# Making the head of the Fourier stage inside the channel MLP's stage

## The reference, cut to what matters

```
x = shortcut + window_attention(ln(x))
x = x + gelu(ln(x) @ fc1_w + fc1_b) @ fc2_w + fc2_b          # channel MLP
g = group_norm(x, 32 groups)                                 # per image: mean, variance, (g - m) / sqrt(s + 1e-5)
f = rfft2(g)                                                 # per image, over the 16 x 16 tokens
o1 = softshrink(f times the complex block weights w1 + b1)   # 8 blocks of 24 channels
o2 = softshrink(o1 times w2 + b2)
x = x + irfft2(o2) + g
```

## Time and profile before

| | us |
|---|---|
| median of 3 runs | 1169.13 |
| lowest and highest run | 1167.31, 1169.83 |
| span of the profiled execution | 1161.7 |
| PE busy in that span | 1005.0 (87%) |

### The profile page before, as it was taken

The page is one execution under the profiler, slowest core; times in us unless marked ns, Lnnn a source line. Parts: engine busy times, 40 slices in busy tenths (PEclk is TensorE's granted clock), DMA queues, the critical chain, the costliest instruction groups (busy, mean ns, idle before and its releaser), DMA issues. The chain is left out here.

```text
span 1161.7 us, 20448 instructions
## 1 busy us (share of the span) xinstructions
PE 1005.0 (87%) x7506; PEld 763.8 (66%) x7507; DVE 574.7 (49%) x1388; ACT 424.4 (37%) x859; POOL 286.9 (25%) x399
## 2 busy tenths in 40 slices
PE   6895999999699699899799659999849799975996
PEld 5685778787465578688698526666637455554675
DVE  4753555653311475456566743444458477642221
ACT  3655155555232223344352111111127276731332
POOL 4454320110100112100001344555412211111242
PEclk9885899999799899899898869999969899985998
DMA  8543763320011120200004611112144433125660
GB/s 91 118 124 120 166 149 80 93 69 3 1 41 62 42 59 1 55 1 2 1 1 119 191 34 41 49 45 52 25 123 108 125 110 93 48 86 200 207 202 14
DMA packets 103286, 91.58 MB, mean 79 GB/s; under 512 B 25873, under 2 KB 95063, under 8 KB 102558
## 3 DMA queue, kind: packets, MB, share of 16 engines
q1 hardware_dynamic: 90953, 75.58, 24.3%
q0 software_dynamic: 5632, 11.07, 3.6%
q10 hardware_dynamic: 6613, 3.74, 1.1%
HBM read 64.44 MB, written 29.70 MB: 81 GB/s over the span
## 5 line engine op out<-in xcount | busy, mean ns | idle before, releaser
L1224 DVE TENSOR_REDUCE l0a_nmax<-l0a_psS 98x2 f32<-98x392 f32 x96 | 54.4, 567 | 55.1 <-PE l0a_psS L1039 51.0
L868 DVE TENSOR_REDUCE l3a_nmax<-l3a_psS 128x2 f32<-128x512 f32 x96 | 62.0, 685 | 31.6 <-PE l3a_psS L722 31.6
L2665 ACT ACTIVATE l2e_H<-l2e_psH 128x512 f32<-128x512 f32 x40 | 21.7, 594 | 129.3 <-PE l2e_psH L2627 129.3
L824 ACT ACTIVATE l3a_PT<-l3a_psST 128x512 f32<-128x512 f32 x96 | 54.6, 596 | 28.7 <-PE l3a_psST L752 28.2
L1174 ACT ACTIVATE l0a_PT<-l0a_psST 98x392 f32<-98x392 f32 x96 | 47.2, 497 | 42.1 <-PE l0a_psST L1081 41.8
L2645 PEld LDWEIGHTS l2e_psY<-W2T,l2e_HT 128*128 128x128 f32 x320 | 51.5, 190 | 15.9 <-issue 15.7
L2588 POOL DMA_INDIRECT ys<-l2e_Y,result_of x40 | 42.0, 1051 | 71.3 <-DVE l2e_Y L2692 65.2
L2645 PE MATMUL l2e_psY<-W2T,l2e_HT 128*128 x320 | 57.3, 332 | 1.3 <-DVE l2e_Y L2692 0.8
L2624 PE MATMUL l2e_psH<-W1T,l2e_XT 128*128 x80 | 41.3, 640 | 2.8 <-issue 2.0
L2583 POOL DMA_INDIRECT l2e_X<-xn,token_at x40 | 39.3, 983 | 17.1 <-issue 17.1
L2692 DVE COPY l2e_Y<-l2e_psY 128x384 f32<-128x384 f32 x20 | 11.2, 558 | 65.1 <-PE l2e_psY L2645 65.1
(11 more groups left out here) (559 smaller groups left out, 2699.9 us busy)
## 6 DMA issues: line engine op xcount, KB each, us to landing
l3w_A<-in_w SPq DMA_DIRECT2D x8, 771.0 KB, 5.4
l3w_B<-in_w SPq DMA_DIRECT2D x8, 672.0 KB, 5.4
l3a_QS<-qd SPq DMA_DIRECT2D x72, 64.0 KB, 2.3
l3a_KS<-kd SPq DMA_DIRECT2D x72, 64.0 KB, 2.3
rd<-l0q_r_p SPq DMA_DIRECT2D x24, 168.0 KB
l0a_QS<-qd SPq DMA_DIRECT2D x54, 64.0 KB
l0a_KS<-kd SPq DMA_DIRECT2D x54, 64.0 KB
W2T<-in_w2t SPq DMA_DIRECT2D x2, 1536.0 KB, 16.9
```

The source lines that it names most:

```text
L824: nc.scalar.activation(PT[n % 3][:, s, :], psST[item % 2][:, :], ACT.Exp).then_inc(exp_done, 1)
L868: nc.vector.tensor_reduce(nmax[k % 2][:, TI * u:TI * (u + 1), s], psS[item % 2][:, :].rearrange("p (t k) -> p t k", t=TI), AX.X, ALU.max, ...
L1224: mx = nc.vector.tensor_reduce(nmax[k % 2][0:WQ, 2 * j:2 * (j + 1), s], psS[item % 2][0:WQ, 0:2 * W0].rearrange("p (t k) -> p t k", t=2), ...
```

## The change

A class `FourierFront` now owns the tiles and semaphores of the group norm (sums, squares, XC, SQ, XN and so on, names l1g_...), of the block weights and of the constant rows. It lives in a stage of its own around the MLP and the Fourier stage, so its tiles keep their places across the barrier. Its methods have the operations of before, unchanged in form. The MLP's stage calls them for pair 0, with its own psT tiles for the products of mean and variance; the Fourier stage calls them for the later pairs only.

```diff
-def l0_mlp(nc, G, w):
+def l0_mlp(nc, G, w, gn, w_next):
...
         def _(sp):
+            gn.load_weights(sp, w_next)
             for p in range(NP - 1):
...
         def _(pool):
+            gn.clear_weights()
             for p in range(NP):
...
                 nc.gpsimd.tensor_tensor(X, X, free(b2[:, 0:1], [0, 4], [1, C]), ALU.add).then_inc(x_biased, 1)
+                if p == 1:
+                    gn.negate_weights(pool)
...
                 first(p)
                 if p + 1 < NP:
                     norm(p + 1)
+                if p == NP - 2:
+                    pe.wait_ge(xT_done, 2 * NP)
+                    gn.mean(pe, psT[0], 0)
+                if p == NP - 1:
+                    gn.variance(pe, psT[1], 0)
                 second(p)
...
                 hidden(p)
                 if p + 1 < NP:
                     norm(p + 1)
+                if p == NP - 2:
+                    gn.square(act, 0)
+                    gn.square(act, 1)
+            gn.root(act, 0)
...
                 if p + 1 < NP:
                     norm(p + 1)
+                if p == NP - 2:
+                    gn.total(dve, 0, (x_in, 16))
+                    gn.centre(dve, psT[0], 0)
+                if p == NP - 1:
+                    gn.square_total(dve, 0)
+                    gn.with_eps(dve, psT[1], 0)
+                    gn.scale(dve, 0)
+                    gn.norm(dve, 0)
                 for a in range(2):
...
+                if p == 0:
+                    gn.constant_rows()
```

More of the change, by code:

```diff
@@ L1259, in _, with __init__, clear_weights, load_weights @@
                         stats.vector(nc, dve, 2 * p + a, a, (x_added, 2 * p + a + 1))
+class FourierFront:
+    def __init__(self, st, G):
+        self.nc, self.G, self.st = st.nc, G, st
+        self.ones = G["afno"]["ones"]
+        two = lambda name, shape: [st.sb(f"{name}{u}", shape) for u in range(2)]
+        self.sums, self.squares = st.sb("sums", [P, 2, GROUPS]), st.sb("squares", [P, 2, GROUPS])
+        self.var, self.std, self.rstd = (st.sb(n, [P, 2, GROUPS]) for n in ("var", "std", "rstd"))
+        self.XC, self.SQ, self.XN = two("XC", [P, TI, C]), two("SQ", [P, TI, C]), two("XN", [P, TI, C])
+        self.sum_done, self.mean_mm, self.xc_done, self.sq_done, self.square_done = st.sems("sum_done mean_mm xc_done sq_done square_done")
+        self.var_mm, self.eps_done, self.std_done, self.rstd_done, self.xn_done = st.sems("var_mm eps_done std_done rstd_done xn_done")
+        R = CH + 1
+        self.W1, self.W2, self.lam = st.sb("W1", [R, 2, 3, CH]), st.sb("W2", [R, 2, 3, CH]), st.sb("lam", [CH, 1])
+        self.FX, self.C1 = st.sb("FX", [R, 2, 2, 2 * NF]), st.sb("C1", [R, 2, 2, 2 * NF])
+        self.w_zeroed, self.w_in, self.negated, self.rows_set = st.sems("w_zeroed w_in negated rows_set")
+    def clear_weights(self):
+        self.nc.gpsimd.memset(self.W1[:], 0.0).then_inc(self.w_zeroed, 1)
+        self.nc.gpsimd.memset(self.W2[:], 0.0).then_inc(self.w_zeroed, 1)
+        self.nc.gpsimd.memset(self.lam[:, :], -LAMBDA).then_inc(self.negated, 1)
+    def load_weights(self, sp, w):
+        W1, W2, R = self.W1, self.W2, CH + 1
+        sp.wait_ge(self.w_zeroed, 2)
+        for n in range(NB):
+            a, k = n // 4, n % 4
+            r = slice(k * BS, (k + 1) * BS)
+            of_block = lambda ap: rows(ap, n * BS * BS, [BS, BS], [NB * BS * BS, 2], [1, BS])
+            sp.dma_start(W1[r, a, 1:3, r], of_block(w["w1"])).then_inc(self.w_in, 16)
+            sp.dma_start(W2[r, a, 1:3, r], of_block(w["w2"])).then_inc(self.w_in, 16)
+        for a in range(2):
+            sp.dma_start(W1[CH:R, a, 1:3, :], rows(w["b1"], a * CH, [C, 1], [C, 2], [1, CH])).then_inc(self.w_in, 16)
+            sp.dma_start(W2[CH:R, a, 1:3, :], rows(w["b2"], a * CH, [C, 1], [C, 2], [1, CH])).then_inc(self.w_in, 16)
+    def negate_weights(self, pool):
+        pool.wait_ge(self.w_in, 16 * (2 * NB + 4))
+        for W in (self.W1, self.W2):
+            self.nc.gpsimd.tensor_scalar(W[:, :, 0, :], W[:, :, 2, :], -1.0, None, ALU.mult).then_inc(self.negated, 1)
+    def constant_rows(self):
+        R, V = CH + 1, self.nc.vector
+        V.memset(self.FX[CH:R, :, :, 0:NF], 1.0).then_inc(self.rows_set, 1)
+        V.memset(self.FX[CH:R, :, :, NF:], 0.0).then_inc(self.rows_set, 1)
+        V.memset(self.C1[CH:R, :, 0, :], 1.0).then_inc(self.rows_set, 1)
+        V.memset(self.C1[CH:R, :, 1, :], 0.0).then_inc(self.rows_set, 1)
+    def mean(self, pe, psM, p):
+        pe.wait_ge(self.sum_done, 2 * p + 2)
+        if p:
+            pe.wait_ge(self.xc_done, 2 * p)
+        self.nc.tensor.matmul(psM[:, 0:2 * GROUPS], self.ones[:, :], self.sums[:, :, :].rearrange("p u g -> p (u g)"), start=True, stop=True).then_inc(self.mean_mm, 1)
+    def variance(self, pe, psV, p):
+        pe.wait_ge(self.square_done, 2 * p + 2)
+        if p:
+            pe.wait_ge(self.eps_done, p)
+        self.nc.tensor.matmul(psV[:, 0:2 * GROUPS], self.ones[:, :], self.squares[:, :, :].rearrange("p u g -> p (u g)"), start=True, stop=True).then_inc(self.var_mm, 1)
+    def square(self, act, i):
+        act.wait_ge(self.xc_done, i + 1)
+        if i >= 2:
+            act.wait_ge(self.square_done, i - 1)
+        self.nc.scalar.activation(self.SQ[i % 2][:], self.XC[i % 2][:], ACT.Square).then_inc(self.sq_done, 1)
+    def root(self, act, p):
+        act.wait_ge(self.eps_done, p + 1)
+        self.nc.scalar.activation(self.std[:], self.var[:], ACT.Sqrt).then_inc(self.std_done, 1)
+    def total(self, dve, p, *ready):
+        for sem, value in ready:
+            dve.wait_ge(sem, value)
+        if p:
+            dve.wait_ge(self.mean_mm, p)
+        for u in range(2):
+            X = self.G["X"][:, TI * (2 * p + u), 0:1]
+            self.nc.vector.tensor_reduce(self.sums[:, u, :], free(X, [GC, GROUPS], [C, TI], [1, GC]), AX.XY, ALU.add).then_inc(self.sum_done, 1)
+    def spread(self, ap):
+        return free(ap, [0, TI], [1, GROUPS], [0, GC])
+    def in_groups(self, ap):
+        return ap.rearrange("p t (g c) -> p t g c", g=GROUPS)
+    def centre(self, dve, psM, p):
+        dve.wait_ge(self.mean_mm, p + 1)
+        for u in range(2):
+            X = self.G["X"][:, TI * (2 * p + u):TI * (2 * p + u + 1), :]
+            self.nc.vector.tensor_tensor(self.in_groups(self.XC[u][:]), self.in_groups(X), self.spread(psM[:, u * GROUPS:u * GROUPS + 1]), ALU.subtract).then_inc(self.xc_done, 1)
+    def square_total(self, dve, p):
+        if p:
+            dve.wait_ge(self.var_mm, p)
+        for u in range(2):
+            dve.wait_ge(self.sq_done, 2 * p + u + 1)
+            self.nc.vector.tensor_reduce(self.squares[:, u, :], free(self.SQ[u][:, 0, 0:1], [GC, GROUPS], [C, TI], [1, GC]), AX.XY, ALU.add).then_inc(self.square_done, 1)
+    def with_eps(self, dve, psV, p):
+        dve.wait_ge(self.var_mm, p + 1)
+        self.nc.vector.tensor_scalar(self.var[:], psV[:, 0:2 * GROUPS].rearrange("p (u g) -> p u g", u=2), 1e-5, None, ALU.add).then_inc(self.eps_done, 1)
+    def scale(self, dve, p):
+        V, std, var, rstd = self.nc.vector, self.std, self.var, self.rstd
+        dve.wait_ge(self.std_done, p + 1)
+        V.reciprocal(rstd[:], std[:]).then_inc(self.rstd_done, 1)
+        dve.wait_ge(self.rstd_done, 4 * p + 1)
+        V.tensor_tensor(std[:], rstd[:], rstd[:], ALU.mult).then_inc(self.rstd_done, 1)
+        dve.wait_ge(self.rstd_done, 4 * p + 2)
+        V.scalar_tensor_tensor(std[:], std[:], -0.5, var[:], ALU.mult, ALU.mult).then_inc(self.rstd_done, 1)
+        dve.wait_ge(self.rstd_done, 4 * p + 3)
+        V.scalar_tensor_tensor(rstd[:], std[:], 1.5, rstd[:], ALU.add, ALU.mult).then_inc(self.rstd_done, 1)
+        dve.wait_ge(self.rstd_done, 4 * p + 4)
+    def norm(self, dve, p, *ready):
+        for u in range(2):
+            for sem, value in ready:
+                dve.wait_ge(sem, value(2 * p + u))
+            self.nc.vector.tensor_tensor(self.in_groups(self.XN[u][:]), self.in_groups(self.XC[u][:]), self.spread(self.rstd[:, u, 0:1]), ALU.mult).then_inc(self.xn_done, 1)
@@ L1413, in afno_tiles, with l1_afno @@
     return [(t["ones"], consts["gnones"]), (t["DF"], consts["dft"]), (t["IV"], consts["idft"]), (t["IVB"], consts["idftb"])]
-def l1_afno(nc, G, w, consts, transfers):
+def l1_afno(nc, G, w, consts, transfers, gn):
     with Stage(nc, "l1") as st:
         NP, R = B // 2, CH + 1
+        W1, W2, lam, FX, C1, negated = gn.W1, gn.W2, gn.lam, gn.FX, gn.C1, gn.negated
         ones, DF, IV, IVB = (G["afno"][n] for n in ("ones", "DF", "IV", "IVB"))
-        W1 = st.sb("W1", [R, 2, 3, CH])
-        W2 = st.sb("W2", [R, 2, 3, CH])
-        lam = st.sb("lam", [CH, 1])
         two = lambda name, shape: [st.sb(f"{name}{u}", shape) for u in range(2)]
[L1429 to L1432, removed]
+        XN, XS, xn_done = gn.XN, two("XS", [P, TI, C]), gn.xn_done
         UP, DN = two("UP", [CH, 2, 2 * NF]), two("DN", [CH, 2, 2 * NF])
@@ L1501, in _ @@
         def _(pe):
```

(20 more changed lines are left out.)

75 lines of the change are left out of this document (8 added, 67 removed).

## The result

The changed kernel takes 1160.69 us (median of 7 runs, 1155.68 to 1164.96), the kernel before 1167.31 beside it (7 runs): ratio 0.9943, interval 0.9921 to 0.9964, so 6.6 us faster. The forecast was 1159.7, or 9.4 us; direction and time are right, but nearly a third of the gain is missing, and where it went is the question of the experiments. The profiled executions are no measure of it: spans of 1161.7 and 1158.5 us differ by 3.2.

What follows compares the result with a forecast made beforehand. PE was taken to limit the MLP and Fourier stage, except for a hole of some ten microseconds between them. Terms -9.98 - 1.82 + 1.6 + 0.8 = -9.4 us took 1169.1 to 1159.7 us, range 1157.5 to 1163.2.

Steps and rivals of the forecast that it cites:

- The chain goes: Head of the Fourier stage: first forward starts when the barrier does, without the group norm's chain in front; 9.98 us removed.
- The start at once: PE's first Fourier product starts with the barrier's release: 0 us taken, up to 3.7 could hide there.
- rival 2: PE stalls at the Fourier stage's barrier for code not yet there, up to 3.7 us; time 1165.2, chance 0.05.
- The clock: First forward pair of the Fourier stage runs at full clock, 4.12 us instead of 5.94; 1.82 us gained.
- Rival 1: The clock falls all the same, so the first forward stays at 5.94 us; time 1161.5, chance 0.12.
- PE waits in the third pair: MLP, before second(2): the product for the means waits for ACT's xT; costs 1.6 us, ends 1.3 and 2.2.
- The memsets: Head of the MLP: two POOL memsets delay DVE's first eight normalisations; costs 0.8 us, ends 0 and 1.16.
- Variance, end of the norm, weights, constant rows, squares: This work, moved into the MLP, fits beside other work or into existing waits; costs 0 us.
- Rivals 3 and 4: Means wait for first pair's round trip, about 1173, chance 0.02; another Fourier engine late in first pair, 1161.7, chance 0.06.
- Sum for the two stages: MLP and Fourier stage together: -9.98 - 1.82 + 1.6 + 0.8 = -9.4 us.
- The range: Whole program between 1157.5 and 1163.2 us, from the terms' ends and the spread of the runs.
- The change ends before 470 us, and the barriers carry the shift through to the end.: Stages behind the Fourier stage: unchanged, so the whole -9.4 us reaches the program's time.

Runs made afterwards that it cites:

- weights_only: Against the kernel before: only weights, negation and constant rows made in the MLP's stage, first pair's group norm left at the Fourier stage's head; ratio 0.9991.
- before_delay: The kernel before with one POOL memset of about 0.3 us put behind the Fourier stage's last statistics; ratio 1.0025 to the kernel before.

## Why the prediction was right, and where it was not

- *The chain goes, 9.98 us.* Forward came 10.0 us behind the barrier, now 0.1. The size is right. That "everything between is the group norm" is not: DVE's four memsets stood in front of the sums (from 387.50 to 389.86), and with them gone and the norm left, in weights_only, forward came at 7.2. The change takes both away, so the sum doesn't feel it. The start at once was right too: rival 2, and with it the Trainium skill's rule on branches (Runtime: NRT & Kernel Launch, Instruction fetch mechanics), is not seen at this barrier; whether the branch's target lay outside the window that the rule speaks of, no run shows.
- *The clock, 1.82 us.* 5.94 less 4.09 is 1.85, at granted clock 1.00. Rival 1 falls.
- *PE waits in the third pair, 1.6 us.* second(2) starts 55.5 us behind the MLP's barrier, before 53.7: 1.79, of which 0.18 was there at second(0) already. 1.6, right.
- *The memsets, 0.8 us.* Mis-sized: 0.30 at the transposes, 0.1 to 0.2 of the whole stage. I scaled a case with memsets of 0.8 each by their length. DVE and POOL shared the loss here; POOL's three memsets took 0.39 longer. The whole 1.16 that I worked out by the Trainium skill's rule (SBUF — State Buffer, Who interferes with whom) is further off still.
- *Variance, end of the norm, weights, constant rows, squares: nothing.* Right: PE's wait before second(3) fell from 1.37 to 1.00 with the product in it, and no new wait appears. Rivals 3 and 4 are not seen either: PE doesn't wait for the sums, and from 394.3 to 410 it is busy 15.70 of 15.70 us.
- *Sum for the two stages:* forecast -9.4, measured -10.0; the difference is, but for 0.1, the memsets' term.
- *The range.* Its low end doesn't follow from its own terms: 1158.6 less the 1.8 of the spread is 1156.8, not 1157.5. The measured 1160.69 lies inside either.
- *"The change ends before 470 us, and the barriers carry the shift through to the end."* This step failed. The shift is carried, but the landmark stage comes to lie otherwise against the clock, and gives 3.2 us back: 10.0 less 3.2 is 6.8, and 6.6 was measured. The prediction had a rival for a clock that falls in the Fourier stage, none for one that falls 92 us into the next stage, in unchanged code. That the time came out inside the range was luck in this respect: the range was wide for other reasons.

## What to carry to other kernels

Work at the head of a stage in which the limiting engine waits can be worth its whole length once all that stands there is moved, and little before: here the norm and the weights each hid the other. Judge such a change stage by stage between barriers, and don't put a later stage down to the change or to chance unseen: here one with a thin stretch of TensorE work (busy 2.5 of 4 us) changed by 3 us when its start moved by tenths of one against the clock. A delay of 0.3 us put into the kernel before is a cheap test of whether a loss elsewhere belongs to the change at all.

## What the runs showed that I had not expected

- A 0.34 us memset in front of a barrier made the program 2.9 us slower (before_delay), by the clock of a stretch 92 us behind it, where three groups of products took 7.6 us instead of 4.3.
- The same stage of unchanged code took 99.8 to 103.0 us over twelve profiles, with its length equal to 0.1 us where the clock's fall lay at 0.45 to 0.48 (three profiles of two kernels) and where it lay at 0.08 to 0.33 (four profiles of three).
- In weights_only PE's first products in the stage came earlier than before, and yet the clock rose only 0.6 us earlier, so the first forward lasted longer, 7.02 against 5.94 us, and took back part of the gain.
